# Attention block and anisotropic spectral filter: the filter network in two batches, and constant tables loaded in two parts

## What is computed

```python
# block 0: attention over the 1024 points of each image
hn = group_norm(x, 16 groups) * norm_w + norm_b
q, k, v = conv1x1(hn, wq/wk/wv) + biases
att = softmax(q^T k * c**-0.5)            # 1024 x 1024 per image
x = x + conv1x1(v att^T, wp) + bp
# block 1: filter in the spectrum, with a 7x7 kernel computed from the image
xf = fftshift(fft2(x, norm='ortho'))
center = abs(xf).mean(channels)[7x7 in the middle]
params = relu(center @ w1 + b1) @ w2 + b2          # 49 -> 32 -> 3
theta = arctan2(p0, p1)/2 + pi/2;  lam1 = exp(p2);  lam2 = 1/(lam1 + 1e-8)
k = exp(-(x_rot**2/(2 lam1**2) + y_rot**2/(2 lam2**2)));  k /= k.sum() + 1e-8
filt = conv 7x7 of real and imaginary parts with k, zero padding
out = real(ifft2(ifftshift(wr @ filt))) + x
```

## Time and profile before

| | us |
|---|---|
| median of 3 runs (455.68 to 458.01) | 456.28 |
| the profiled execution | 458.12 |
| its span, first to last instruction | 456.30 |

### The profile page before, as it was taken

The page is one execution under the profiler, slowest core; times in us unless marked ns, Lnnn a source line. Parts: engine busy times, 40 slices in busy tenths (PEclk is TensorE's granted clock), DMA queues, the critical chain, the costliest instruction groups (busy, mean ns, idle before and its releaser), DMA issues.

```text
span 456.3 us, 7030 instructions
## 1 busy us (share of the span) xinstructions
PE 411.3 (90%) x2263; PEld 344.7 (76%) x2263; DVE 317.2 (70%) x575; ACT 253.6 (56%) x450; POOL 233.8 (51%) x176
## 2 busy tenths in 40 slices
PE   2669999999999999999999999999964089999995
PEld 2447788888888888888888888888744088888884
DVE  3569698768849967894995888478343833577765
ACT  1557676656747665784664677467512312355451
POOL 0566457636816754781673476276013512467562
PEclk9999999999999999999999999999989555699999
DMA  6900100100010010010001001002150000111112
GB/s 171 385 29 2 47 1 0 47 0 0 8 38 0 0 46 0 0 46 0 0 0 46 0 0 47 1 1 68 48 134 0 0 1 1 43 49 46 76 63 92
DMA packets 6094, 17.54 MB, mean 38 GB/s; under 512 B 1632, under 2 KB 2272, under 8 KB 5856
## 3 DMA queue, kind: packets, MB, share of 16 engines
q1 hardware_dynamic: 4784, 16.70, 10.7%
q10 hardware_dynamic: 1296, 0.66, 0.5%
HBM read 13.16 MB, written 4.19 MB: 38 GB/s over the span
## 4 chain that ended last, share of the span: by engine, by line
PE 84%; DVE 8%; ACT 4%; issue 1%; DMA 1%; POOL 1%
PE PS L386 63%; PE PS L452 11%; PE PS L506 7%; PE PS L497 2%; DVE NMX L1081 1%; PE PS L528 1%; ACT E L815 1%; DMA X<-in_x 1%; DVE ETL L1096 1%; DVE K L1354 1%; DVE ML L1286 1%; DVE STAT L992 1%; ACT ETH L824 0%; ACT ETH L945 0%; POOL E L1450 0%
## 5 line engine op out<-in xcount | busy, mean ns | idle before, releaser
L1450 POOL TENSOR_TENSOR E<-E,RI 128x1024 f32<-128x1024 f32 x64 | 124.6, 1948 | 112.2 <-DVE RI L1086 112.2
L1081 DVE TENSOR_REDUCE NMX<-PS 128x1 f32<-128x1024 f32 x64 | 77.9, 1216 | 35.1 <-PE PS L386 34.5
L815 ACT ACTIVATE E<-PS,NMX 128x1024 f32<-128x1024 f32 x64 | 71.5, 1117 | 36.5 <-DVE NMX L1081 36.3
L824 ACT ACTIVATE ETH<-PS 128x512 fp32r<-128x512 f32 x128 | 69.5, 597 | 34.8 <-PE PS L452 34.4
L1096 DVE TENSOR_TENSOR ETL<-PS,ETH 128x512 fp32r<-128x512 f32 x128 | 82.0, 681 | 8.5 <-ACT ETH L824 7.7
L452 PE MATMUL PS<-MISC,E 128*128 128x128 f32 x512 | 67.2, 274 | 3.7 <-POOL E L1450 2.7
L452 PEld LDWEIGHTS PS<-MISC,E 128*128 128x128 f32 x512 | 58.7, 140 | 14.8 <-POOL E L1450 5.9
L386 PE MATMUL PS<-ETH,VH 128*128 128x512 f32 x128 | 55.1, 431 | 0.4 <-DVE ETL L1096 0.4
L386 PE MATMUL PS<-ETH,VL 128*128 128x512 f32 x128 | 50.9, 397 | 0.0
L386 PE MATMUL PS<-ETL,VH 128*128 128x512 f32 x128 | 50.5, 395 | 0.0
L386 PE MATMUL PS<-KH,QH 128*128 128x512 f32 x128 | 41.5, 406 | 2.1 <-ACT E L815 1.2
(11 more groups left out here) (188 smaller groups left out, 788.9 us busy)
## 6 DMA issues: line engine op xcount, KB each, us to landing
XTF<-in_xt SPq DMA_DIRECT2D x8, 512.0 KB, 3.3
X<-in_x SPq DMA_DIRECT2D x7, 512.0 KB, 9.3
out<-X SPq DMA_DIRECT2D x7, 512.0 KB, 2.6
E<-in_gam SPq DMA_DIRECT2D x1, 1488.4 KB, 8.9
R<-in_ana SPq DMA_DIRECT2D x1, 1320.0 KB, 5.6
E<-in_syn SPq DMA_DIRECT2D x1, 752.0 KB, 4.5
X<-in_x ACTq DMA_DIRECT2D x1, 512.0 KB, 4.6
XTF<-in_syn SPq DMA_DIRECT2D x1, 512.0 KB, 5.3
```

Source lines behind the costliest of these rows:

```text
L815: act.activation(E[:, (t % 4) * N:(t % 4 + 1) * N], s_bank(t), ACT.Exp, bias=NMX[:, t % 2:t % 2 + 1], accum_out=RS[:, t % 4:t % 4 + 1]).th ...
L824: act.activation(et[:, h, 4 * k:4 * k + 4, i * P:(i + 1) * P], bank(ET_BANK + k).rearrange("p (j n) -> p j n", j=4), ACT.Copy).then_inc(s[ ...
L1081: dve.tensor_reduce(NMX[:, t % 2:t % 2 + 1], s_bank(t), AX.X, ALU.max, negate=True)\
L1450: TT(e, e, RI[:, t % 4:t % 4 + 1].broadcast_to([P, N]), ALU.mult)\
```

## The change

**Network in two batches.** `BATCHES` are images 0 to 5 and 6, 7. Batch 0 runs inside pass 7, the last with both attention and a previous image: GpSimd takes the magnitudes (squares, sum, a floor, and a power of one half in place of ScalarE's root) behind `scale(7,1)`, PE gets `centre`, `hidden` and `parameters` at tiles 4 and 5, VectorE `mlp_size` and `mlp_norm` at tile 6 and `mlp_sign` to `mlp_exponent` at tile 7, GpSimd `root(0)`, ScalarE `scale_exp` and `kernel_exp`. Batch 1 is spread in the same pieces over steps 0 to 3.

**Tail.** Pass 8 is replaced by `last()` on each engine, in which the tail of image 7, the border products of batch 0 in four parts, and the head of the synthesis (image 0's rt, r3, khat, v3, vt) are interleaved. `synthesis` has no hardware loop any more. The block copy for v3 is done by ScalarE.

**Tables.** The split is made on the host; high and low parts come as separate arrays. They are transferred from fp32 into fp32r tiles from the GpSimd queue: ANH and ANL in pass 0 at tile 2, `gam` in pass 7 at tile 7 (into the room of Q and K), SYH and SYL in `last()`.

```diff
@@ attention / synthesis
-            run(B, False, True, False)
-        def synthesis(first, step, eng):
-            first()
-            step(0, 3)
-            with eng.Fori(1, B - 3) as i:
-                step(i, 3)
-            for i in range(B - 3, B):
+        def synthesis(step):
+            for i in range(B):
                 step(i, B - 1 - i)
@@ SP
-            sp.dma_start(R[:, 0:UW], ana).then_inc(s["d_ana"], 16)
-            sp.dma_start(SYF, syn[:, 0:T_COS]).then_inc(s["d_syn"], 16)
-            sp.dma_start(COSF[:], syn[:, T_COS:T_END]).then_inc(s["d_syn"], 16)
-            sp.dma_start(E[0:K_ROWS, 0:GAM + NK * NK], gam).then_inc(s["d_gam"], 16)
@@ PE
+            def last():
+                p, pv, o = B - 1, LAST_PV_BANK, bank(LAST_U_BANK)
+                kernel_sum(0)
+                values(p, 0, 2)
+                kernel_thirds(0)
+                transposes(p, 7)
+                values(p, 0, 3)
+                borders(0, 0)
+                values(p, 1, 0, pv=pv)
+                out_project(p, 0, False)
+                borders(0, 1)
+                values(p, 1, 1, pv=pv)
+                x1_transposes(p, 0)
+                borders(0, 2)
+                values(p, 1, 2, pv=pv)
+                rt(0)
+                borders(0, 3)
+                khat(0, 0)
+                values(p, 1, 3, pv=pv)
+                pe.wait_ge(s["v_xl"], 2 * p + 1)
+                for t in TILE_ORDER[:TILES // 2]:
+                    features(t, o)
+                out_project(p, 1, False)
+                r3(0, after_mix=False)
+                pe.wait_ge(s["v_g"], 3)
+                khat(0, 1)
+                x1_transposes(p, 1)
+                v3(0)
+                vt(0)
+                pe.wait_ge(s["v_xl"], 2 * p + 2)
+                for t in TILE_ORDER[TILES // 2:]:
+                    ins = features(t, o)
+                ins.then_inc(s["p_u"], 1)
+                rt(1)
             def step(i, more):
+                if i == 3:
+                    pe.wait_ge(s["v_o"], 6)
+                    borders(1, 0)
                 z(i, 0)
                 if more:
                     r3(i + 1, after_mix=is_later(i))
+                if i == 0:
+                    centre(1)
+                if i == 2:
+                    pe.wait_ge(s["v_o"], 4)
+                    kernel_sum(1)
+                if i == 3:
+                    borders(1, 1)
                 z(i, 1)
...
@@ DVE, image
+                    if not nxt and t == 5:
+                        hidden_copy(0)
...
+                    if not nxt and t == 5:
+                        params(0)
...
+                    if not nxt and t == 6:
+                        mlp_size(0)
+                        mlp_norm(0)
+                    if not nxt and t == 7:
+                        mlp_sign(0)
+                        mlp_angle(0)
+                        mlp_axes(0)
+                        mlp_exponent(0)
                 if prev:
                     misc_lo(XTL[:, 4:8, :], XTH[:, 4:8, :], "a_xh", 2 * p + 2, "v_xl")
@@ POOL
+                    if not nxt and t == 7:
+                        pool.wait_ge(s["p_s"], TILES * B)
+                        pool.dma_start(QK[0:K_ROWS, 0:GAM + NK * NK], gam).then_inc(s["d_gam"], 16)
...
+                    if not nxt and t == 7:
+                        root(0)
                     if cur:
                         scale(b, t)
+                    if not nxt and t == 1:
+                        magnitude(0)
...
+                    if not prev and t == 2:
+                        pool.dma_start(ANH[:], anh).then_inc(s["d_ana"], 16)
+                        pool.dma_start(ANL[:], anl).then_inc(s["d_ana"], 16)
+            def magnitude(k):
+                pool.wait_ge(s["a_ur"], BATCHES[k][0] + BATCHES[k][1])
+                f = FR[:, images(k), :]
+                TT(f, f, f, ALU.mult).then_inc(s["g_m2"], 1)
...
+                TT(f[:, :, NF:2 * NF], f[:, :, 0:NF],
+                   HALF_POWER[:].rearrange("p (a b) -> p a b", a=1)
+                   .broadcast_to([P, BATCHES[k][1], NF]), ALU.pow).then_inc(s["g_mag"], 1)
+            def last():
+                p = B - 1
+                rst(0)
+                pool.wait_ge(s["p_pv"], 2 * p + 1)
+                pool.dma_start(SYH, syh).then_inc(s["d_syn"], 16)
+                pool.dma_start(SYL, syl).then_inc(s["d_syn"], 16)
+                pool.memset(G3S, 0.0).then_inc(s["g_g3z"], 1)
+                keep_x1(p, 0)
+                rst(1)
+                k_x1(0, 0)
+                keep_x1(p, 1)
+                k_x1(0, 1)
+                magnitude(1)
+                rst(2)
```

More of the change, by code:

```diff
@@ L168, in shape_tables @@
     g = ((g + g[::-1]) / 2)[:NF]
[L169 to L171 removed]
+    gam = np.zeros((K_ROWS, GAM + NK * NK), np.float32)
+    thirds(gam, *halves(g))
     misc = np.zeros((P, M_END))
@@ L750, in step @@
                     khat(i + 1, 1)
-                    vt(i + 1)
+                if i == 0:
+                    hidden(1)
+                if i == 3:
+                    borders(1, 2)
+                if more:
+                    vt(i + 1)
+                if i == 0:
+                    parameters(1)
+                if i == 2:
+                    kernel_thirds(1)
+                if i == 3:
+                    borders(1, 3)
                 mix(i, 0, last=more == 0)
@@ L962, in first @@
                 rt_hi(1)
+            attention(image, act)
+            last()
             def step(i, more):
+                if i == 2:
+                    kernel_exp(1)
                 if more:
@@ L979, in step @@
                 if more > 1:
+                    g3_copy(i + 2)
                     rt_hi(i + 2)
-            synthesis(first, step, act)
+                if i == 2:
+                    thirds_hi(1)
+            synthesis(step)
         @block.vector
@@ L1383, in first @@
                 g_full(0)
+                out_lo(p, 1, LAST_PV_BANK)
+                g3_columns(0)
                 g_lo(0)
-                g3_columns()
-                g3_copy(0)
+                residual(p, 1)
+                misc_lo(XTL[:, 4:8, :], XTH[:, 4:8, :], "a_xh", 2 * p + 2, "v_xl")
                 v3_lo(0)
                 g_full(1)
-                g3_copy(1)
                 vt_lo(0)
                 rt_lo(1)
+            attention(image, dve)
+            last()
             def step(i, more):
+                if i == 4:
+                    dve.wait_ge(s["v_g"], 6)
@@ L1401, in step @@
                     z_lo_last(1)
+                if i == 0:
+                    hidden_copy(1)
+                if i == 1:
+                    mlp_sign(1)
                 if more:
@@ L1412, in step @@
                 result(i, 1)
-            synthesis(first, step, dve)
+                if i == 0:
+                    mlp_norm(1)
+                if i == 1:
+                    mlp_exponent(1)
+            synthesis(step)
         @block.gpsimd
@@ L1534, in step @@
                     rst(i + 3)
-            synthesis(first, step, pool)
+                if i == 0:
+                    root(1)
+            synthesis(step)
 _ORDER = ["x", "L0_conv_norm_w", "L0_conv_norm_b", "L0_conv_wq", "L0_conv_bq", "L0_conv_wk",
```

516 lines of the change are left out of this document (287 added, 229 removed).

## The result

The changed kernel takes 498.96 us (median of 4, 494.88 to 499.39), the kernel before 457.14 beside it; the ratio is 1.0875, 95% interval 1.0838 to 1.0913. The profiled execution took 498.91 us for a span of 497.1. The forecast was 443.5: even its sign was wrong.

What follows compares the result with a forecast made beforehand. The prediction took the order of PE's queue as the bound, TensorE being busy 90% of the span. First synthesis product at 364.0, plus 68.8 of synthesis and 10.7 for batch 2, gave 443.5 us; range 430 to 461.

Steps and rivals of the forecast that it cites:

- (a): GpSimd, magnitude(0) behind scale(7,1): power on 150 elements 5.8 us, bounds 0.9 and 53; PE late by 3.5 us.
- the rival: Slower power on GpSimd, scale(7,2) queued behind it: gain gone at 0.12 us per element, 468 us at 0.2; chance 0.12.
- The second batch's power: Synthesis steps: centre(1) on PE waits 1.0 us for magnitude(1).
- the clock term: PE after the 5 us wait before analysis(6): half-rate issue costs +1.7 us, bounds 0 and +25.
- (b): PE, image 7: centre(0), hidden(0), parameters(0) add about 1.0 us and a wait near 0.9; +1.9 us.
- (c): VectorE, image 7: small network instructions, held by GpSimd, delay the last row maximum and XTL's low part; +7.0 us.
- The first product: First synthesis product on PE at 364.0 us, where it was 380.53; analysis(6) starts at 331.4.
- The synthesis: First synthesis product to the end: 68.8 us at full clock, plus 10.7 for batch 2 in steps 0 to 3.
- The waits inside steps 0 to 3: Batch 2's waits on PE in the first synthesis steps: 6.4 us with centre(1)'s 1.0, bounds 2 and 10.
- Rival 3: Tail: the clock stays low, PE's 27.7 us there run at half rate, giving 468 us; chance 0.06.

Runs made afterwards that it cites:

- e1: The changed kernel with both powers on GpSimd replaced by a plain copy, the root left out; 459.32 us (10 runs).
- e4: e3 with XTL's low part of image 6 made on VectorE ahead of mlp_sign to mlp_exponent; 456.65 us, ratio 0.9963.
- e10: The changed kernel with its three longest PE waits filled by 134 useless products; 488.28 us (4 runs).
- e6: e4 with batch 1's pieces placed a step later and batch 0's small VectorE chain behind the splits; 442.87 us, ratio 0.9566.
- e3: The changed kernel with the magnitudes' root on ScalarE in place of the power on GpSimd; 461.01 us, ratio 1.0066.
- e7: The kernel before with only gam split on the host and cast by two transfers from GpSimd's queue; 445.83 us, ratio 0.9709.
- e8: e7 with 29 useless products on PE ahead of its waits for the magnitudes and the exponential kernel; 441.98 us, ratio 0.9736.

## Why the prediction was wrong

**(a) The power, the step that failed.** The prediction bracketed the power on 150 elements by 0.9 and 53 us and took 5.8 inside the bracket, with a tenth of the single element's price per element, 0.035 us, since "most of its time should be start-up". It is 0.16: magnitude(0)'s power took 24.3 us, and PE's wait was 22.3, not 3.5. The formula 24.3 + 1.5 - 3.8 = 22.0 gives that wait, so the mechanism and the place (scale(7,2) queued behind it) were right and only the size was off. The reason given was even true: 0.38 of the 0.54 us of one element is start-up. What did not follow from it was the tenth; the remaining 0.16 us is 4.5 times the 0.035 taken, and by the rival's own break-even, 0.12 us per element, it decides for slower. One row of one size could not tell start-up from price per element, and nothing on record spoke for a tenth; the rival that rests on this had a chance of 0.12.

The second batch's power is the same step again: centre(1) was given 1.0 us of wait and took 7.2. With 0.16 in both places the forecast would have been 443.5 + 18.8 + 6.2 = 468.5 us. The rest, up to a span of 497.1, is the clock term below. The forecast also set the median equal to the span, while an execution takes 1.8 us more than its span.

**(b) and (c), right.** Without the power the forecast for analysis(6) is 331.4 - 3.5 = 327.9, and e1 has 327.89. That it fits so closely is luck: PE waited 0.26 us for hidden_copy(0) and not 0.9, and 0.6 us lost at the low clock stands in for it. The large parts are right: 2.0 us in front of the transposes of tile 6, where 2.5 was foreseen behind mlp_size and mlp_norm, and 4.7 for XTL, where it was 3.5 + 1.4 - 0.4 = 4.5. In the changed kernel PE's wait for XTL was 4.9 us; e4 removed 4.0. VectorE's small instructions were held by GpSimd as foreseen; of the changed kernel:

```profile
340.29 1.38 DVE L1373 SCALAR_TENSOR_TENSOR ML<-ML 49x12 f32<-49x12 f32 x1
...
346.78 1.75 DVE L1404 TENSOR_SCALAR ML<-ML 49x6 f32<-49x6 f32 x1
```

**The first product, right but for the clock.** 364.0 - 3.5 = 360.5 forecast, 362.73 in e1, where windows of 1 us between analysis(6) and there give 3.8 us lost to the low level against the 1.7 taken. In the changed kernel analysis(6) to z(0,0) is 34.8 us for a forecast of 32.6, with 3.7 lost.

**The synthesis, wrong by the clock.** From z(0,0) to the end the forecast was 68.8 + 10.7 = 79.5 us. e1, the same order with no power at all, needs 95.3, of which windows of 1 us put 15.3 down to the clock, so 80.0 without: at full clock the sum was good. The changed kernel needs 110.2: 6.2 more for the second power, and 26 at the low clock between 385 and 465. Its steps 0 to 3 take 462.31 - 386.94 = 75.4 us, where 45 was foreseen; from step 4 on the steps are 8.7 and 8.5 us long, as foreseen.

```profile
462.31 0.57 PE L396 MATMUL PS<-ETH 112*128 112x512 f32 x1
```

The waits inside steps 0 to 3, apart from centre(1), were counted as 5.4 us. The changed kernel shows 5.1: 2.55 for rt_lo's ETL (foreseen 3.8), and these:

```profile
425.07 0.23 PE L396 MATMUL PS<-ML,MISC 49*49 49x2 f32 x2 [0.81 <-ACT ML L1004]
...
437.41 0.80 PE L396 MATMUL PS<-ETH,WH 128*128 128x512 f32 x1 [0.94 <-DVE K L1207]
...
439.85 0.35 PE L396 MATMUL PS<-K,QK 96*112 96x4 f32 x1 [0.78 <-DVE X L1248]
```

The last two are thirds_lo(1) and result(2,1), foreseen at 0.9 and 0.7; the first, kernel_sum(1) waiting for the exponential, was not foreseen.

**The clock term, the second failure.** The prediction took 1.7 us for the clock and let the 16.5 us that it costs before vanish with the gap behind which it stood. It is 33.1 in the changed kernel and 20.3 without the powers. The 14.8 us of clock that the forecast counted as won never came. Of the 53.6 us by which the span missed the forecast, the powers' waits are 25.0 and the clock 31.4, other terms giving 2.8 back; 12.8 of the clock's part goes with the powers, 18.6 stays without them. The reason given, that the clock stays low where PE had stood idle for long, was half of it: e10 confirms it for the long waits, but e1 and e6 show falls in steps that have small waits or none. What brings them about is not shown; narrow products stand at each of them, but also in steps that keep the clock. Rival 3 priced the low clock at 25 us for the tail; the tail kept its clock (360 to 385 us at 0.98) and the steps lost it.

**What the change is worth without the power.** e3, ratio 1.0066: nothing. Idle time falls by 9 us, work grows by 7 and the clock's cost by 5. What the rearrangement needed is in e4 to e6. e7, which has none of it, takes 12 to 13 us off before by the split of one table on the host. e6, with everything, is 3 us faster than e7 by the medians and 1.4% (6.5 us) by the ratios, whose intervals, 0.9505 to 0.9627 and 0.9681 to 0.9737, don't meet. So most of the gain that can be had belongs to the table, and the two batches add a few us, only with the root on ScalarE and after three further moves.

Open: why the same kernel, e6 for one, keeps 0.984 in one execution and 0.960 in another; what, beside long waits, brings the clock down in the steps; and whether filling would pay more with narrow products packed into fewer wide ones.

## What to carry to other kernels

A time at one size does not tell start-up from price per element: before a bracket of 0.9 to 53 us is narrowed, look for or measure a second size. Here one element at 0.54 us agreed with both ends, while 2 and 6 elements together (0.168 us per element) would have given 25 us. Never move such a function to an engine whose next work the bound engine waits for without a break-even beside its worst end. When a gap on PE is removed, the low clock behind it is not yet won back: look at what PE streams there, since in a step with short waits and narrow products it can be 1.2 GHz while the busy share says 100%. And compare kernels whose clock wanders by several executions of each: a profile is one of them.

## What the runs showed of the hardware

- GpSimd's power costs 0.16 us per element of a row and about 0.38 us once, from 1 to 150 elements, while the neighbouring plain operation on 150 took 0.47 us.
- A VectorE tensor_scalar with one SBUF input, of 49x6, took 1.75 us while GpSimd scaled a tile (346.61 to 348.50), where its neighbours took 0.16. The prediction had reckoned only with two-input instructions. The Trainium skill (SBUF — State Buffer, "Who interferes with whom") lists tensor_scalar among those that can enter a two-port mode and are then shut out; the trace agrees.
- Granted clock: 1.2 GHz for 30 us with PE nearly full (430 to 460 of the changed kernel), and falls with no idle time in the 5 us before (365 and 410 of e6). Behind the same wait of 2.8 us it fell in e7's profiled execution (0.75 and 0.57 in 330:340) and not in e8's (1.00). The Trainium skill (TensorE: Matmul & The Clock Gate, "A second HAM failure mode: psum-queue depth-cycling") tells of a kernel whose clock swung between its two levels because PE paused briefly and often between groups of products. Here e1's fall at 401, behind waits of 0.94 and 0.78 us, agrees with it; e6's fall at 365 has no pause ahead of it.
- Casting transfers from GpSimd's queue, fp32 in memory to fp32r tiles (issue, KB, us to landing), of the changed kernel:

```profile
QK<-in_gam POOLq DMA_DIRECT2D x1, 1488.4 KB, 9.1
ANH<-in_anh POOLq DMA_DIRECT2D x1, 1320.0 KB, 6.1
ANL<-in_anl POOLq DMA_DIRECT2D x1, 1320.0 KB, 9.8
ETH<-in_syh POOLq DMA_DIRECT2D x1, 1264.0 KB, 5.8
ETL<-in_syl POOLq DMA_DIRECT2D x1, 752.0 KB, 7.0
```

The first is as fast as the plain one of the earlier trace rows (9.1 us against 8.9). ANL and SYL are issued right behind ANH and SYH and land later, 9.8 and 7.0 us after their issue. khat(0,0) didn't wait for them, and the 0.5 us taken for them was not needed; nor did the analysis table's two cost anything, scale(7,1) starting at 295.37 us where it was 295.49. Each costs GpSimd 0.5 to 0.8 us to issue.
